# Parting VectorE's two first sums of a unit: one behind the first maximum of step 2, one behind the second

## The reference

```python
qkv = x @ w_qkv                                 # 16 heads of 32
scores = einsum('bnqd,bnkd->bnqk', q, k) / sqrt(512)
ctx = einsum('bnqk,bnkd->bnqd', softmax(scores), v)
x = layernorm(x + ctx)
gate, up = fp4_linear(x, w_gate), fp4_linear(x, w_up)      # 1408 wide, blocks of 16 in FP4
x = layernorm(x + fp4_linear(silu(gate) * up, w_down))
```

## Time and profile before

| what | us |
|---|---|
| median of 3 runs | 3721.09 (3719.73 to 3721.95) |
| the profiled execution's own time | 3722.25 |
| its span in the trace | 3720.5 |
| PE busy | 3569.6 (96%) |
| DVE busy | 3035.9 (82%) |
| POOL busy | 2484.8 (67%) |
| ACT busy | 1740.4 (47%) |

### The profile page before, as it was taken

How to read it: one execution, slowest core, us unless ns; L and a number is a source line. 1 busy time by engine, 2 the same in 40 slices (tenths; PEclk the granted TensorE clock), 3 DMA queues, 4 the chain that set the end, 5 groups by cost and what they waited for, 6 DMA issues and landing times.

```text
span 3720.5 us, 58214 instructions
## 1 busy us (share of the span) xinstructions
PE 3569.6 (96%) x21226; PEld 1562.3 (42%) x21226; DVE 3035.9 (82%) x4562; ACT 1740.4 (47%) x3072; POOL 2484.8 (67%) x1626
## 2 busy tenths in 40 slices
PE   4799999999999999999999999999999999999898
PEld 2334444334443344343444344433444334444244
DVE  9877898778977789778987789877898778877687
ACT  3466523664246632565236652366424663255522
POOL 2289655885569855797458865588555985569744
PEclk9899999999999999999999999999999999999999
DMA  5211233022321234111431223302232122311022
GB/s 184 89 29 35 69 87 86 18 50 79 93 62 31 45 94 97 45 30 39 113 96 31 41 66 90 86 18 49 75 95 65 29 48 73 73 42 28 1 75 65
DMA packets 412462, 234.55 MB, mean 63 GB/s; under 512 B 331152, under 2 KB 357776, under 8 KB 412048
## 3 DMA queue, kind: packets, MB, share of 16 engines
q1 hardware_dynamic: 412176, 230.82, 24.4%
HBM read 72.09 MB, written 32.24 MB: 28 GB/s over the span
## 4 chain that ended last, share of the span: by engine, by line
PE 70%; DVE 10%; issue 8%; POOL 4%; DMA 1%; ACT 1%; SPq 1%; DVEq 0%; POOLq 0%; ACTq 0%
PE SC L1768 18%; PE CT L1732 9%; PE R L727 7%; PE SC L1717 7%; DVE mx L633 7%; PE R L707 7%; PE R L1768 6%; PE R L1790 6%; PE CT L1790 6%; PE R L739 2%; PE R L717 2%; POOL wd L1293 2%; PE R L749 1%; POOL x L1293 1%; DVE split L627 1%
## 5 line engine op out<-in xcount | busy, mean ns | idle before, releaser
L633 DVE TENSOR_REDUCE mx<-R 128x1 f32<-128x512 f32 x2048 | 1282.5, 682 | 283.7 <-PE R L727 282.3
L1438 ACT ACTIVATE arena<-SC 128x512 f32<-128x512 f32 x1364 | 754.4, 603 | 395.0 <-PE SC L1717 330.5
L1768 PE MATMUL SC<-wgu,split 128*128 128x512 f16 (+1 forms) x3456 | 705.5, 361 | 5.3 <-DMA split<-split 5.3
L1293 POOL TENSOR_TENSOR wd<-wd,arena 128x1024 f32<-128x1024 f32 x216 | 514.5, 2408 | 93.3 <-DVE wd L1574 59.2
L1768 PEld LDWEIGHTS SC<-wgu,split 128*128 128x128 f16 x3456 | 337.4, 98 | 356.1 <-DMA split<-split 7.7
L1438 ACT ACTIVATE wd<-SC 128x512 f32<-128x512 f32 x684 | 385.4, 603 | 204.1 <-PE SC L1717 175.0
L1327 POOL TENSOR_TENSOR arena<-arena,sc_h 128x512 f32<-128x512 bf16 (+2 forms) x144 | 178.0, 1250 | 420.3 <-DVE arena L556 420.3
L707 PE MATMUL R<-xT,wqkv 128*128 128x512 bf16 x1536 | 399.6, 381 | 7.5 <-DVE split L627 6.4
L1481 ACT ACTIVATE arena<-SC,gain 128x512 f32<-128x512 f32 (+1 forms) x192 | 125.0, 651 | 584.0 <-PE R L1768 301.6
L727 PE MATMUL R<-ks_even,qs_even 96*128 96x512 bf16 x1024 | 378.8, 384 | 20.1 <-DVE mx L633 10.2
L727 PE MATMUL R<-arena 96*128 96x512 bf16 x1024 | 381.6, 382 | 8.5 <-DVE split L627 4.1
(11 more groups left out here) (151 smaller groups left out, 5245.8 us busy)
## 6 DMA issues: line engine op xcount, KB each, us to landing
x<-n_L_attn_embeddings_dram SPq DMA_DIRECT2D x72, 256.0 KB, 3.3
wd<-wd_kept SPq DMA_DIRECT2D x32, 512.0 KB, 4.6
out_dram<-x SPq DMA_DIRECT2D x64, 256.0 KB, 2.9
ks_even<-split SPq DMA_DIRECT2D x192, 64.0 KB, 2.0
qs_even<-split SPq DMA_DIRECT2D x384, 32.0 KB, 1.9
arena<-split SPq DMA_DIRECT2D x192, 64.0 KB, 2.0
arena<-split SPq DMA_DIRECT2D x384, 32.0 KB, 1.9
arena<-n_L_attn_embeddings_dram SPq DMA_DIRECT2D x48, 256.0 KB, 3.8
```

Of the source, the lines that this page charges most:

```text
L633: nc.vector.reduce_max(mx[:, j:j + 1], ring_of(ring, job)[:, :], AX_X).then_inc(max_done, 1)
L1293: nc.gpsimd.tensor_tensor(acc[u % 2][i], acc[u % 2][i], probs_of(s)[:, hs, :], ALU.add).then_inc(pool_sum, 1)
L1438: nc.scalar.activation(probs_of(s)[:, hd, :], SC[e % SLOTS][:, :], ACT.Exp, scale=SCALE).then_inc(exp_done, 1)
L1768: last = nc.tensor.matmul(GU[kk % 2][which][:, 0:w], xhT[i % 2][:, part_x * KH + k, :], wgu[:, part_w * KH + k, which * I + first:which * ...
```

## The change

Sum A moves from behind maximum 11 to behind maximum 10; sum B stays behind maximum 11. The work is the same. The waits at the head of `first_sums` now stand in both calls. The last unit of all keeps its order.

```diff
-FIRST_SUM_STEP, FIRST_SUM_MAX = 2, 2
+FIRST_SUM_STEP, FIRST_SUM_MAX = 2, (1, 2)
...
-                def first_sums(u):
+                def first_sums(u, halves=range(2)):
...
-                    for i in range(2):
+                    for i in halves:
...
-                                if t == FIRST_SUM_STEP and n_max == FIRST_SUM_MAX:
-                                    first_sums(u)
+                                if t == FIRST_SUM_STEP and n_max in FIRST_SUM_MAX:
+                                    first_sums(u, [FIRST_SUM_MAX.index(n_max)])
```

## The result

| | us |
|---|---|
| before, median of 4 runs | 3721.02 (3719.73 to 3721.95) |
| changed, median of 4 runs | 3798.54 (3795.81 to 3803.7) |
| ratio | 1.0208 [1.0196, 1.0221] |
| changed, profiled execution: time, span | 3799.64, 3797.9 |

What follows compares the result with a forecast made beforehand. PE bounds the f32 weighings, DVE the maxima behind the sums. Eight batches lose 60 us, kinds 6 and 7 about 3, less some regained: 60 taken, so 3722.25 becomes 3782, median 3781, range 3748 to 3797.

Steps and rivals of the forecast that it cites:

- Sum A 0.60 us earlier, POOL with it: Step 2 of kind 0: sum A starts at 629.17, not 629.77, and POOL is released 0.60 us earlier, at 630.56.
- Maximum 11 later at no cost: Its reduction on DVE moves back 1.14 us; PE's block of matmuls covers this, so it was priced at nothing.
- More waits and queues: One to four more DVE waits per unit, on events long past: 3 us at the most, taken as 0.
- Sum B stands behind POOL's addition, 3.09 us long and 1.87 late: Kind 0: sum B, wanted at 630.91, stands until POOL's addition ends at 632.92 and ends at 634.00, not 632.13.
- 42 units: Units where sum A releases POOL: kinds 0, 2, 3, 4, 5 in eight batches, kinds 6 and 7 in the first.
- What a late sum B costs the end: 1.87 us less DVE's idle time: kinds 0, 2, 3, 4, 5 lose 1.6, 1.35, 1.32, 1.35, 1.87; eight batches lose 60.
- The clock: TensorE's granted clock behind the new wait in kinds 0 and 5: the prediction had no term for it.
- all 42 units lose the whole 1.87: Upper case for the range: every affected unit loses all of sum B's lateness, 3721 + 79 = 3800 us.
- absorbed: Rival 1: PE's idle waits, the maxima's DMA or POOL's chain absorb the delay; 0 to 0.5 us a unit, some 3731; chance 0.07.
- not met: Rival 2: POOL starts later or sum B gets ahead, so the lock is not met; 3718 to 3722 us; chance 0.05.
- faster: Rival 3: at the `sum` job in kinds 3 and 5, PE gets up to 9.6 us back, 3712; chance 0.03.
- The sign named for them: In the profile: sum B keeping 1.22 us refutes the lock step; 3 us with time under 3735 refutes DVE to PE.

Runs made afterwards that it cites:

- the repeat: The changed kernel run once more without any edit, beside the run with eight more matmuls in kind 5 alone on the same chip: 3802.58 us, ratio 1.0212.
- the filler in kinds 0 and 5: Changed kernel plus eight more matmuls remaking maximum 14's score tile before PE's wait in kinds 0 and 5: 3793.8 us; same addition to the kernel before: 3745.39 us.

## Why the prediction was wrong, point by point

- *Sum A 0.60 us earlier, POOL with it*: right; POOL started 0.18 us after sum A's end (641.73 against 640.34 + 1.21), 0.17 before.
- *Maximum 11 later at no cost*: right, and shown for twice the lateness by the run with both sums behind maximum 10.
- *More waits and queues*: right; the run with one wait more on POOL, which has all the waits of the changed kernel, is within 4 us.
- *Sum B stands behind POOL's addition, 3.09 us long and 1.87 late*: right: 3.05 to 3.10 us in 40 of the 42 units, 3.34 and 3.35 in the others, and 1.84 to 1.89 late where it is read at maximum 12 in kinds 0 and 5 (2.13 in the last batch's kind 5). It rested on one row of this shape and one pair of another.
- *42 units*: right, counted.
- *What a late sum B costs the end*: mis-sized, but not what made the forecast too low. Kinds 2 and 4 have 1.05 for 1.35, kind 3 1.18 for 1.32: I counted DVE's idle time of 0.23 us as 0.23 us of room. Instructions that follow without a wait overlap by 0.09 us in the records (0.69 long, 0.60 apart), so each such gap has 0.32 to give: 1.87 - 0.16 - 0.32 - 0.32 = 1.07. The same 0.09 on kind 3's 0.55 gives 1.23. In kind 0 I took 0.29 off for the slack at maximum 21; the chain to maximum 22 had none (1.88). These errors cancel in part: 58 us in place of 63, of which I took 60.
- *The clock*: this is the step that failed. The prediction let PE go on at its old speed behind the new wait; the loss from the clock stood at nothing, without a word on it. It had 1.6 us for kind 0 and 1.87 for kind 5, where the changed kernel pays 3.2 and 4.1. The forecast of 3781 and the measured 3798.5 differ by 17.5, and 19 us lie in the stretches at the lower clock; that the other terms came out 2 us too high hid a little of it. The range's upper end stood on "all 42 units lose the whole 1.87", which takes the lateness as a ceiling; it is none if the wait that it causes makes the engine behind it slow. That the measured 77.5 us lie next to 42 x 1.87 = 79 is chance: kinds 2, 3 and 4 lose less than 1.87 and kinds 0 and 5 more.
- *Rivals*: absorbed, not met, faster: none of them. The sign named for them (sum B near 3 us, in 42 units) settles it for the lock.

## What to carry to other kernels

When VectorE and GpSimd both work on SBUF, two VectorE operations with two SBUF inputs that stand back to back keep GpSimd out between them; one that is put behind a PSUM reduction (0.60 us here, where GpSimd started 0.18 us after the first sum's end) gives GpSimd the time to start and then waits for its whole instruction. Either keep them together, or let GpSimd wait for both: here the first cost nothing that can be told and the second 4 us (0.1%), while the parting cost 77 us (2%). And where a change adds a wait to a TensorE that was busy without a break (1.87 to 2.38 us here), look at the granted clock behind it before taking the wait as the ceiling of the loss.

## What the runs showed of the hardware that was not expected

- PE's wait of 1.87 to 2.38 us for a ring bank in kinds 5 and 0 was often met by a stretch of 3.4 or 6.8 us at a granted clock of 0.50 (thirteen stretches in 16 such units, and thirteen again in the repeat). In kind 0 of batches 1, 4 and 6 the same wait of 2.37 or 2.38 us was followed by none. Waits of 1.19 us (kind 1 of the run with sum B behind maximum 12) and 1.28 us (kind 5 of the run parted in kinds 0 and 5) were followed by a stretch in some units, and 1.49 us in kind 3 of the changed kernel in none. So the length of the wait doesn't decide alone; what does, these runs don't tell.
- Eight matmuls more per unit, of no use for the result, made the changed kernel 16 us faster (3786.3 against 3802.6 us) when placed in kind 5's wait; some of it may be kind 0's stretches, which differ between executions.
- With the filler in kinds 0 and 5, a transposing DMA at the next stage's start took 5.0 us to land in place of 2.7; this landing was read in the kernel before with the filler, and in the changed kernel with the filler PE's waits for that DMA are longer too (2.0 to 2.4 us in the first five batches). The cause is open.
